# Squared distances moved from a stage of their own into the groups of the experts' stage

## The reference, cut to what matters

```
x = x + ffn(layernorm(x), ...)                       # experts
# alignment of ctx (small) with layernorm(x) (large), for each of 64 sequences
aa = sum(ctx * ctx, -1)[:, None];  bb = sum(xn * xn, -1)[None, :]
D  = sqrt(maximum(aa + bb - 2.0 * ctx @ xn.T, 0.0))  # 128 x 128
R  = dtw_cost(D)       # row by row: r = d + min(up, left, diagonal)
path = backtrack(R);   x = x + small rows gathered along the path
```

## Time and profile before

| | |
|---|---|
| median of 3 runs (lowest, highest) | 3513.56 us (3511.64, 3516.18) |
| profiled execution, its span | 3515.2 us, 3513.5 us |
| busy share of the span, PE, DVE, ACT, POOL | 89%, 69%, 53%, 38% |
| attention | 0 to 1841 us |
| experts | 1841 to 2736.9 us |
| distances | 2737 to 2834 us |
| alignment with the way back | 2834 to 3031 us |
| convolution network | 3031 to 3513.5 us |

### The profile page before, as it was taken

How to read it: one execution, slowest core, us unless ns; L and a number is a source line. 1 busy time by engine, 2 the same in 40 slices (tenths; PEclk the granted TensorE clock), 3 DMA queues, 4 the chain that set the end, 5 groups by cost and what they waited for, 6 DMA issues and landing times. The chain is left out here.

```text
span 3513.5 us, 64326 instructions
## 1 busy us (share of the span) xinstructions
PE 3133.3 (89%) x23332; PEld 2709.4 (77%) x23332; DVE 2410.9 (69%) x5382; ACT 1869.6 (53%) x4845; POOL 1344.9 (38%) x1116
## 2 busy tenths in 40 slices
PE   6999999999999999999988999999999832277776
PEld 5888888888888888888876888888888720155554
DVE  6666666666666666666656566565665878699997
ACT  5565555655555565555543333333333544299986
POOL 2333333333333333333322333333333200078887
PEclk9999999999999999999998999999999965598898
DMA  4000000000000000000002110101101660001100
GB/s 153 5 8 7 5 7 4 7 4 7 7 4 8 4 8 5 7 4 8 4 5 75 49 44 31 50 29 46 49 25 50 193 131 0 18 25 42 37 31 31
DMA packets 112376, 107.99 MB, mean 31 GB/s; under 512 B 24256, under 2 KB 93376, under 8 KB 112064
## 3 DMA queue, kind: packets, MB, share of 16 engines
q1 hardware_dynamic: 112064, 103.88, 10.3%
HBM read 90.75 MB, written 13.11 MB: 30 GB/s over the span
## 5 line engine op out<-in xcount | busy, mean ns | idle before, releaser
L671 POOL TENSOR_TENSOR attention_prob<-attention_prob,attention_inv_sums 128x1024 f32<-128x1024 f32 x256 | 479.7, 1895 | 408.8 <-DVE attention_inv_sums L565 408.8
L442 ACT ACTIVATE attention_prob<-attention_turns,attention_neg_max 128x256 f32<-128x256 f32 x1024 | 467.6, 482 | 174.5 <-DVE attention_neg_max L556 174.5
L1120 POOL TENSOR_TENSOR experts_hidden_lo<-experts_weighed,experts_hidden_hi 128x512 fp32r<-128x512 f32 x192 | 252.0, 1313 | 550.5 <-ACT experts_hidden_hi L943 550.5
L572 DVE COPY attention_probT<-attention_turns 128x512 f32<-128x512 f32 x512 | 328.7, 684 | 169.4 <-PE attention_turns L329 169.3
L556 DVE TENSOR_REDUCE attention_neg_max<-attention_turns 128x2 f32<-128x512 f32 x512 | 317.7, 682 | 45.4 <-PE attention_turns L319 44.4
L943 ACT ACTIVATE experts_hidden_hi<-experts_weighed 128x512 fp32r<-128x512 f32 x192 | 121.3, 632 | 423.3 <-DVE experts_weighed L1072 423.3
L433 ACT COPY attention_v<-attention_turns 128x512 f32<-128x512 f32 x256 | 150.9, 590 | 315.8 <-PE attention_turns L263 315.8
L329 PEld LDWEIGHTS attention_turns<-ident,attention_prob 128*128 128x128 f32 x2048 | 240.2, 141 | 39.7 <-POOL attention_prob L671 4.2
L329 PE MATMUL attention_turns<-ident,attention_prob 128*128 128x128 f32 x2048 | 266.1, 273 | 3.7 <-POOL attention_prob L671 3.7
L1067 DVE TENSOR_TENSOR experts_silu<-experts_silu,experts_spread 128x512 f32<-128x512 f32 x128 | 89.8, 702 | 258.9 <-ACT experts_silu L937 257.9
L345 PE MATMUL attention_heads_out<-attention_probT,attention_v 128*64 128x128 f32 x4096 | 253.5, 277 | 0.8 <-DVE attention_probT L572 0.8
(11 more groups left out here) (274 smaller groups left out, 9822.8 us busy)
## 6 DMA issues: line engine op xcount, KB each, us to landing
experts_spread<-shares SPq DMA_DIRECT2D x256, 128.0 KB, 3.0
attention_ctx<-in_ctx SPq DMA_DIRECT2D x32, 256.0 KB, 2.7
distance_ctx<-in_ctx SPq DMA_DIRECT2D x16, 512.0 KB, 4.3
distance_ctxT<-in_ctxT SPq DMA_DIRECT2D x32, 256.0 KB, 4.8
weights_ctx<-in_ctx SPq DMA_DIRECT2D x16, 512.0 KB, 3.8
out<-conv_x_out SPq DMA_DIRECT2D x15, 512.0 KB, 3.0
x_all<-in_x SPq DMA_DIRECT2D x7, 1024.0 KB, 9.5
dist<-distance_dist SPq DMA_DIRECT2D x16, 256.0 KB, 2.5
```

Source lines behind the costliest of these rows:

```text
L442: made = act.activation(prob[n % 2][:, h, :], bank_of("s", 2 * n + e)[:, m * 256:(m + 1) * 256], ACT.Exp, bias=neg_max[:, n % 2, 2 * e + m ...
L572: dve.tensor_copy(probT[n % 2][:, 2 * g:2 * g + 2].rearrange("p h t c -> p (h t c)"), bank_of("t", 2 * n + g)[:, :]).then_inc(p_copied, 1)
L671: pool.tensor_tensor(prob[n % 2][:, :, :], prob[n % 2][:, :, :], inv[:, n % 2, :].unsqueeze(2).broadcast_to([P, QH, 2 * TOK]), ALU.mult).t ...
L1120: pool.tensor_tensor(hid_lo[n % 3][:, :], weighed[n % 2], hid_hi[n % 3][:, :].bitcast(F32), ALU.subtract).then_inc(hid_split, 1)
```

## The change

The stage `distances` is gone. Its work for group g - 1 is done inside group g of the experts' stage, once `add_out` has finished x there, and for the last group behind the loop:

- DVE: `measure_far` at t = 3, `norm_far` at t = 6 (which also makes the norm of xn from variance and rstd), `copy_far` at t = 7 and 8, `add_norms` at t = 11. POOL takes the power at t = 3. PE transposes at t = 7 and 8 and multiplies at t = 10, in one further bank `far_ps`. ACT clamps at t = 11. The buffers `xn` and `xT` serve both uses.
- The norms of xn go through DRAM (`norms`) and come back spread over all partitions, into the space of `xn`. The products with ones, and ACT's squares, are gone. The norms of ctx come from attention's statistics, two small DVE operations for each pair of sequences.
- For the next group, measuring (t = 1) and normalising (t = 2) are now apart, the transposes stand at t = 4 and 5, the scores at t = 6, routing at t = 7 to 11, `low_x` on POOL at t = 6.
- `spread` is a ring of 6 buffers instead of 8. `dist` holds squared distances; the alignment's ACT takes the roots in place, 8 rows at a time, 5 rows before DVE needs them.

```diff
 # attention, DVE, norm_c(p)
+                mean, var = mv[0][:, 2:4, 0], mv[0][:, 2:4, 1]
+                dve_step(dve, dve.scalar_tensor_tensor(mean_part[:, :], mean, float(DIM), mean, ALU.mult, ALU.mult))
+                dve.scalar_tensor_tensor(ctx_norm[:, 2 * p:2 * p + 2], var, float(DIM), mean_part[:, :], ALU.mult,
+                                         ALU.add)
 # experts, SP
+            def spread_norms(g):
+                sp.wait_ge(far_normed, g + 1)
+                sp.dma_start(norms[0, :].rearrange("(t b) -> t b", b=GB), far_norm[:, 1, :]).then_inc(norms_stored, 16)
+                sp.wait_ge(norms_stored, 16 * (g + 1))
+                sp.wait_ge(far_turned, 2 * g + 2)
+                sp.dma_start(norm_rows, norms.broadcast_to([P, GB * TOK])).then_inc(norms_loaded, 16)
+            def store_far(g):
+                sp.wait_ge(clamped, g + 1)
+                sp.dma_start(dist[GB * g:GB * g + GB].rearrange("b i j -> i b j"), far[:, :, :]
+                             ).then_inc(far_stored, 16)
             for g in range(NG):
...
                 for m in range(TILES):
-                    if g:
-                        sp.wait_ge(silu_weighed, TILES * (g - 1) + m + 1)
+                    j = g * TILES + m
+                    if j >= RING:
+                        sp.wait_ge(silu_weighed, j - RING + 1)
...
+                if g:
+                    spread_norms(g - 1)
+                    store_far(g - 1)
+                for k in range(KD):
+                    sp.dma_start(far_cT[:, k, :, :], ctxT[GB * g:GB * g + GB, k * P:(k + 1) * P, :].rearrange(
+                        "b p t -> p b t")).then_inc(ctx_loaded, 16)
 # experts, PE
+            def turn_far(g, k):
...
+                for i in range(GB):
+                    made = pe.transpose(far_ps[:, i * P:(i + 1) * P], xn[:, i, k * P:(k + 1) * P], ident[:, :])
+                made.then_inc(far_turned, 1)
+            def multiply(g):
+                pe.wait_ge(ctx_loaded, 32 * (g + 1))
+                pe.wait_ge(far_copied, 2 * g + 2)
+                for i in range(GB):
+                    cols = slice(i * TOK, (i + 1) * TOK)
+                    for k in range(KD):
+                        made = pe.matmul(far_ps[:, cols], far_cT[:, k, i, :], xT[:, k, cols], start=k == 0,
+                                         stop=k == KD - 1)
+                made.then_inc(multiplied, 1)
 # experts, ACT
+            def clamp(g):
+                act.wait_ge(far_summed, g + 1)
+                act.activation(far[:, :, :], far[:, :, :], ACT.Relu).then_inc(clamped, 1)
 # experts, DVE
+            def norm_far(g):
+                dve.wait_ge(far_rstd_made, g + 1)
+                dve.wait_ge(turned, 2 * min(g + 3, NG))
...
+                dve_step(dve, dve.scalar_tensor_tensor(far_norm[:, 0, :], far_mv[:, :, 1], float(DIM), far_rstd[:, :],
+                                                       ALU.mult, ALU.mult))
+                tt(far_norm[:, 1, :], far_norm[:, 0, :], far_rstd[:, :], ALU.mult)
+                for i in range(GB):
+                    made = ts(xn[:, i, :], x_all[:, GB * g + i, :], far_mv[:, i, 0:1], far_rstd[:, i:i + 1],
+                              ALU.subtract, ALU.mult)
+                made.then_inc(far_normed, 1)
+            def copy_far(g, k):
+                dve.wait_ge(far_turned, 2 * g + k + 1)
...
+                ts(xT[:, k, :], far_ps[:, :], -2.0, None, ALU.mult).then_inc(far_copied, 1)
+            def add_norms(g):
+                dve.wait_ge(multiplied, g + 1)
+                dve.wait_ge(norms_loaded, 16 * (g + 1))
...
+                for i in range(GB):
+                    cols = slice(i * TOK, (i + 1) * TOK)
+                    made = dve.scalar_tensor_tensor(far[:, i, :], far_ps[:, cols],
+                                                    ctx_norm[:, GB * g + i:GB * g + i + 1], norm_row[:, i, :],
+                                                    ALU.add, ALU.add)
+                made.then_inc(far_summed, 1)
...
+            measure_far(NG - 1)
+            norm_far(NG - 1)
+            for k in range(KD):
+                copy_far(NG - 1, k)
+            add_norms(NG - 1)
 # align, ACT; DVE waits for rooted at each eighth row
+            def root(p):
+                for c, (a, b) in enumerate(LOADS):
+                    if PIECE * p == a:
+                        act.wait_ge(loaded[c], 32)
+                a = 1 + PIECE * p
+                b = min(a + PIECE, SLOTS)
...
+                    made = act.activation(cost[:, a:b, 1:], cost[:, a:b, 1:], ACT.Sqrt)
...
+            root(0)
             for t in range(N):
                 hand_over(t)
+                if t % PIECE == 3:
+                    root(t // PIECE + 1)
```

More of the change, by code:

```diff
@@ L686, in attention, with experts @@
             block.gpsimd(pool_program)
-def experts(nc, dve_step, pool_step, x_all, ident, half, router, bias, gate, up, down, s_gate, s_up, s_down, shares):
+def experts(nc, dve_step, pool_step, x_all, ident, half, router, bias, gate, up, down, s_gate, s_up, s_down, shares,
+            ctx_norm, ctxT, dist, norms):
     TILES = ROUTED // P
@@ L692, in experts @@
     STAGES = 3
+    RING = 2 * STAGES
     with Stage(nc, "experts") as st:
@@ L780, in spreads, with far_in @@
             return g * TILES + max(0, t - STILES)
+        def far_in(n, tile):
+            g, t = divmod(n, per)
+            return g - 1 if t == tile and 0 < g < NG else None
         def is_routed(n):
@@ L1089, in dve_program @@
                 g, t = divmod(n, per)
+                if far_in(n, 6) is not None:
+                    norm_far(far_in(n, 6))
+                for k in range(KD):
+                    if far_in(n, 7 + k) is not None:
+                        copy_far(far_in(n, 7 + k), k)
+                if far_in(n, 11) is not None:
+                    add_norms(far_in(n, 11))
                 if n < N:
```

311 lines of the change are left out of this document (114 added, 197 removed).

## The result

The changed kernel takes 3478.44 us (median of 4 runs, 3476.19 to 3478.94), 0.9899 of the kernel before (95% interval 0.9881 to 0.9916): 35 us less. The forecast was 3472, with a range from 3462 to 3488. Each kernel was profiled in one execution.

What follows compares the result with a forecast made beforehand. PE was taken to bound the experts' groups 1 to 15 (busy 799.77 of 803 us). Terms -80.3 + 40.2 - 3.5 + 1.8 = -41.8 us took 3515.2 to 3473.4, median 1.6 lower: 3472 us, range 3462 to 3488.

Steps and rivals of the forecast that it cites:

- term 1: Distance stage: it goes, 94.6 us, and a tail of 14.3 us for the last group stays: -80.3 us.
- term 4: Alignment: a table load and two roots ahead of row 0, partly taken up by row 8's earlier wait: +1.8 us.
- Term 2: Experts' groups: 8 transposes and 16 product pieces more on PE in each of 15 groups, nothing hidden: +40.2 us.
- The 15 short waits of the earlier trace: Groups 1 to 15: all of PE's waits, 2.8 us together, read as showing that PE bounds the stage.
- Term 3: DVE's order in the groups: about 6 us more a group at cost 0; first group's weighing comes earlier: -3.5 us.
- the slack: DVE between tile 7 and tile 0: 2.3 us left before the down projection is due, so PE does not wait.
- Each later root fits ahead of the next copy: Alignment: a row takes 0.55 us and a copy is needed two rows later, so later roots of 0.63 fit.
- After its wait as before: Alignment, ahead of row 0: ACT loads the root's table only after its wait, 1.28 us on the path.
- Attention, cost 0: Attention: 62 small DVE operations stand where DVE idles, cost 0; 11 us if no idle time took them.
- A: Rival, 14%: further collisions on DVE between tiles 7 and 0 make PE wait: +15 to +30 us, 3487 to 3502.
- B: Rival, 4%: loads of ctx in SP's queue delay the shares' spread by 3.5 us a group: 52 us, 3524 us.
- C: Rival, 5%: PE keeps its clock in the tail and the first group gains 4.2 us: 3465 to 3468.

Runs made afterwards that it cites:

- e10: e2 with the alignment's roots left out, so that it runs on squared distances: 3463.97 us, 0.9858 of the kernel before.
- e11: e6 with 28 filler products on PE between the last down projection and the last group's transposes: 3461.46 us, 0.9850 of the kernel before.
- e2: The changed kernel with mean_part allocated last in the attention instead of in the midst: 3470.19 us, 0.9872 of the kernel before.
- e4: The kernel before with only the new order of the next group's normalisation and routing, distances in their own stage: 3505.32 us, 0.9970.
- e7: e2 with the four sums of add_norms made three times over on DVE: 3485.24 us, 0.9917 of the kernel before.
- e3: The changed kernel without the two DVE operations per pair for the norms of ctx, a constant in their place: 3476.97 us, 0.9891 of the kernel before.
- e1: The kernel before with only the new buffers ctx_norm and mean_part allocated and never used: 3522.84 us, 1.0022.
- e5: e2 with padding that moves only the kv buffers, from place 32 to 0 within 64 B: 3481.71 us, 0.9908 of the kernel before.
- e9: e2 with 32 B of padding ahead of wq, moving every attention buffer by 32 B: 3469.60 us, 0.9871 of the kernel before.
- e8: e2 with padding that moves only wq, wkv and wo, from place 32 to 0 within 64 B: 3473.39 us, 0.9883 of the kernel before.
- e6: e2 with 32 B of padding ahead of attT_hi, so attT lies at 32 within 64 B: 3463.93 us, 0.9856 of the kernel before.
- e12: e11 with filler products in the attention's last round and the last group's norms loaded into a free buffer: 3461.38 us, 0.9852 of the kernel before.

## Why the prediction was right, and where not

**The direction and the large term.** The tail (term 1 with the front of term 4) was forecast at -77.9 us and came to -78.2. Inside, two errors in part cancel: the chain to the clamp is 14.9 for 14.3, and the roots cost 1.35 in front for 2.4 (e10). The half rate of PE behind a pause, which the forecast took from the distance stage, was right (3.75 us for 3.5), and e11 shows that the pause is its cause. How near the total came is in part luck: the attention's +11.2 and the groups' -5.7 were both unforeseen and half cancel. With the attention's pairs put right the kernel takes 3470.2 us (e2), 2 below the forecast.

**Term 2.** Mis-sized by 0.9 only: 39.3 us for 40.2, measured against e4. "Nothing hides it, since PE has no gap" holds for the new work.

**The 15 short waits of the earlier trace rows.** This is the step that failed in the groups. The forecast read them and used them to say that PE is full, but did not ask whether they stay. The new order ends routing a tile earlier, and they go: the order alone gives -4.8 us, a term of the sum that was missing (e4). The list of waits gave 2.8 us, PE's idle time in the earlier trace rows 3.2, and 1.6 are not explained; in e7, too, the list showed less than the time lost.

**Term 3.** Cost 0 in the groups was right, and so, nearly, was the slack: about 2.1 us by e7, for 1.9 reckoned (2.3, less 0.4 for the true sums). DVE's work was put too low, though. Lines of DVE in groups 1 to 15 of the changed kernel (busy us, mean ns of one):

```profile
L1195 DVE TENSOR_SCALAR experts_xn<-x_all,experts_far_mean_var,experts_far_rstd 128x256 f32<-128x256 f32 x60 | 51.1, 916 | 0.0
...
L1216 DVE SCALAR_TENSOR_TENSOR experts_far<-experts_far_ps,ctx_norm,experts_xn 128x128 f32<-128x128 f32 x60 | 22.2, 433 | 0.5
L1206 DVE TENSOR_SCALAR experts_xT<-experts_far_ps 128x512 f32<-128x512 f32 x30 | 20.7, 692 | 9.4 <-PE experts_far_ps L941 8.7
```

The normalisation takes a mean of 916 ns each, and of 407 in the tail, with POOL idle. That collision with POOL was foreseen for this place and not for the copies: those are 692 ns in the groups and 0.69 us in the tail, and the sums 433 and 427 ns. By the Trainium skill, "SBUF — State Buffer", section "Who interferes with whom", a tensor_scalar in a two-port mode and an instruction of POOL shut each other out for the whole instruction, and a DVE instruction outside these modes with at most one input from SBUF does not collide. The trace agrees, with the normalisation for the first kind and the copies and sums, which read PSUM, for the second. DVE has 9.7 us more a group ((634.58 - 488.36) / 15), not 6, in places with time to spare. 0.9 of it is the next group's normalisation, which now meets POOL as well (652 ns for 408). The first group: PE's waits there, of the changed kernel (total us, times, longest).

```profile
PE experts_gate L889 <- ACT experts_silu L1021: 1.6, 1, 1.6
PE experts_up L889 <- DVE experts_weighed L1168: 1.0, 1, 1.0
```

The wait for the weighing fell from 3.93 to 1.0 us, the 2.9 that the rows gave. The 0.6 that the forecast added for the clock came from no row, and the group is 2.8 us shorter; the wait for ACT's silu grew from 0.3 to 1.6 us (0.5 in e4, where the group is 3.5 shorter).

**Term 4.** +1.8 was forecast against a kernel without roots, 3.0 to 3.4 came (e10). (The text of the term has 0.3 us for row 8 and its sum 0.4.) "Each later root fits ahead of the next copy" is wrong: rows 8 to the last take 112.42 us with roots and 111.08 without. "After its wait as before" is wrong too, in the other direction: the table load is hidden. The whole stretch from the first scan came out right (-0.9 for -0.6) because the network behind the alignment was 2.4 us shorter. From the alignment's last row on, the fourteen profiles take 556.2 to 558.8 us; 558.8 is the kernel before, and no experiment says why, so this agreement is luck.

**Attention, cost 0.** The failed step of most weight. The two operations do cost nothing (e3: a pair stays the same without them). But the sum counted instructions and not places: 32 B in the midst of the buffers cost 0.28 us a pair, 8.4 us in all (e1, e2, e5, e9). The other 2.8, 1.1 at the start and 1.7 in the last pair, no experiment ties to the change. The upper bound of 11 us that stood there came from the operations, and had the right size by accident.

Of the rivals, A is about 2 us of DVE work a group away (e7), B did not come (neither PE nor DVE has a wait for the shares' DMA in groups 1 to 15), C did not come: the first group gave 2.8 us and not 4.2, and the tail's clock is 0.57 (1.00 only by the edit of e11). The errors add up: +11.2 (attention) - 5.7 (groups) + 0.7 (first group) - 0.3 - 0.3 = +5.6, and -41.8 + 5.6 = -36.2, for 36.3 measured.

## What to carry to other kernels

A new buffer moves all behind it. Where PE is full, compare the mean time of unedited products before and after, and allocate small late additions last. Ask of each short wait that stands in a full engine's list whether the edit removes it. And give a pause of PE ahead of a serial tail something to do, if the clock falls there.

## What the runs showed of the hardware

- Products of 256 fp32 columns in the q projections ran at 276 ns mean with both SBUF operands at the same place within 64 B, and at 279 to 282 with one of them 32 B off (e5, e8, e9), with PE busy throughout; 12 such products make a q projection, and four projections a pair. For the output's products this is less clean (284 to 288). The products of 512 columns moved by at most 4 ns of some 400, up and down (`wkv_hi` by `kv_hi` 415 in the kernel before and in e5, 417 in e8), and the transposes of `prob`, 128 columns, by less than 1 of 272 when `prob` alone moved by 32 B (e1).
- PE's clock fell to 0.50 in 6.34 us without work (e6) and was at 1.00 when the same stretch was filled (e11). In the attention's last pair the same work, from the last addition of the pair before to its own first, took 41.9 us in e1, with the clock at 1.00 throughout, and 45.8 in the changed kernel, with the clock at 0.50 from 1834.1 to 1847.8 us. What decides between the two stays open (e12); one profile a kernel can't tell the kernel from the execution.
- An ACT table load ran while its queue's next instruction still waited for a DMA, and cost nothing on the path (changed kernel, 2797.35 us; e10). In the earlier trace rows a load stood behind the wait of 2.58 us ahead of its root. What decides which comes first, no run shows.
